# Router logits straight on the tokens, and the preparation of a group spread over thirteen tile steps instead of eleven

## What is computed

```python
xn = _layernorm(x, axis=-1)                     # x: 6250 tokens x 256
x = x + gnn(xn, src, dst, ...) + mix(xn[None], ...)[0]
x = x + ffn(_layernorm(x, axis=-1)[None], ...)[0]

def gnn(h, edge_row, edge_col, W, attn_fc, ln_gamma, ln_beta, ffn_w, ffn_b):
    # attention over 200000 edges gives h_new, then
    h_new = (h_new - mu) * rsqrt(var + eps) * ln_gamma + ln_beta
    return relu(h_new @ ffn_w + ffn_b)

def ffn(x, gamma, beta, Wr, br, W1, b1, W2, b2):  # 8 experts, 2 per token
    xn = (x - mu) * rsqrt(var + eps) * gamma + beta
    logits = einsum('bsd,de->bse', xn, Wr) + br
    top_vals, top_idx = top_k(logits, 2)
    w = softmax(top_vals)
    # y = sum over the two experts e of w_e * (gelu(xn @ W1[e] + b1[e]) @ W2[e] + b2[e])
```

## Time and profile before

| | us |
|---|---|
| timed runs, median of 3 (lowest to highest) | 4579.16 (4575.05 to 4580.97) |
| profiled execution, its own time | 4535.56 |
| span of that execution, first to last instruction | 4533.7 |
| mean granted TensorE clock | 0.82 |
| TensorE busy, in the whole span | 3115.7 (69%) |
| VectorE busy | 2756.3 (61%) |
| ScalarE busy | 1949.4 (43%) |
| GpSimd busy | 2177.1 (48%) |

### The profile page before, as it was taken

The page is one execution under the profiler, slowest core; times in us unless marked ns, Lnnn a source line. Parts: engine busy times, 40 slices in busy tenths (PEclk is TensorE's granted clock), DMA queues, the critical chain, the costliest instruction groups (busy, mean ns, idle before and its releaser), DMA issues.

```text
span 4533.7 us, 80190 instructions
## 1 busy us (share of the span) xinstructions
PE 3115.7 (69%) x17657; PEld 2171.6 (48%) x17657; DVE 2756.3 (61%) x6375; ACT 1949.4 (43%) x5742; POOL 2177.1 (48%) x2438
## 2 busy tenths in 40 slices
PE   4888366666676666677777677776776454777895
PEld 2443133333343433365555555555555333665785
DVE  8999866566676766665555565565555465434322
ACT  4777233233333333344444444444444222544674
POOL 5877555555555555554444444444443532123123
PEclk8888677787788887788888888887888777988998
DMA  2222333434444444433333333333332333334344
GB/s 67 98 96 88 93 102 102 108 102 101 116 108 104 121 100 107 112 93 88 83 83 86 84 91 84 92 88 82 88 83 77 94 113 131 109 106 150 96 137 135
DMA packets 326432, 452.92 MB, mean 100 GB/s; under 512 B 79021, under 2 KB 261483, under 8 KB 326053
## 3 DMA queue, kind: packets, MB, share of 16 engines
q0 software_dynamic: 85552, 236.37, 19.2%
q1 hardware_dynamic: 217896, 194.32, 14.9%
q10 hardware_dynamic: 22860, 20.83, 1.6%
HBM read 366.49 MB, written 84.82 MB: 100 GB/s over the span
## 4 chain that ended last, share of the span: by engine, by line
PE 26%; DVE 22%; issue 19%; another core or an unknown queue 16%; DVEq 7%; ACT 4%; POOL 2%; ACTq 1%; DMA 1%; SPq 1%; POOLq 0%
PE bank L2044 7%; DVE room L1580 4%; PE bank L2228 4%; PE bank L2240 4%; DVEq L1539 3%; PE bank L2078 2%; DVE room L1373 2%; DVE room L1563 2%; DVE room L1372 2%; PE bank L2089 2%; DVE room L1533 1%; DVE room L1553 1%; PE bank L2053 1%; ACT room L1174 1%
## 5 line engine op out<-in xcount | busy, mean ns | idle before, releaser
L883 POOL DMA_INDIRECT room<-table,room x1564 | 1521.1, 973 | 1558.2 <-DVE room L1563 1087.1
L2044 PE MATMUL bank<-room 128*128 128x260 f32 x3520 | 1053.2, 449 | 441.0 <-DVE room L1563 246.5
L2044 PEld LDWEIGHTS bank<-room 128*128 128x128 f32 x3520 | 750.0, 225 | 607.1 <-issue 484.1
L1563 DVE TENSOR_TENSOR room<-room,bank 128x1024 f32<-128x1024 f32 x440 | 534.3, 1214 | 68.5 <-issue 38.6
L1580 DVE TENSOR_TENSOR room<-bank,room 128x1024 f32<-128x1024 f32 x392 | 477.0, 1217 | 133.3 <-remote 69.5
L1174 ACT ACTIVATE room<-bank 128x512 f32<-128x512 f32 (+1 forms) x588 | 251.1, 487 | 372.1 <-remote 291.1
L1553 DVE TENSOR_REDUCE room<-bank 128x32 f32<-128x128 f32 x440 | 124.6, 283 | 438.0 <-remote 251.2
L1106 ACT ACTIVATE bank<-room 128x16 f32<-128x16 f32 x440 | 80.6, 183 | 683.3 <-DVE room L1557 429.9
L1099 ACT ACTIVATE spare<-away,ones 128x512 bf16<-128x512 bf16 x440 | 317.6, 722 | 56.1 <-ACT away L1096 7.9
L2053 PE MATMUL bank<-room 128*33 128x512 f32 (+1 forms) x1568 | 293.6, 480 | 41.6 <-issue 33.8
L2078 PE MATMUL bank<-ident,room 128*128 128x128 f32 x1764 | 296.0, 322 | 34.3 <-issue 23.1
(11 more groups left out here) (319 smaller groups left out, 4939.0 us busy)
## 6 DMA issues: line engine op xcount, KB each, us to landing
spare<-rows_dram SPq DMA_DIRECT2D x440, 128.0 KB
room<-table,room POOLq DMA_INDIRECT x1564
kv_dram<-room SPq DMA_DIRECT2D x49, 324.0 KB, 2.2
room<-kv_dram SPq DMA_DIRECT2D x196, 81.0 KB
y_dram<-planes SPq DMA_DIRECT2D x119, 128.0 KB
room<-xs_dram ACTq DMA_DIRECT2D x110, 128.0 KB
q_dram<-room SPq DMA_DIRECT2D x49, 192.0 KB, 1.9
room<-q_dram SPq DMA_DIRECT2D x196, 48.0 KB
```

The lines of the kernel that those rows point to most:

```text
L883: pool.indirect_dma_start(G[:, k.slot, u, :], None, table, bass.IndirectOffsetOnAxis(ap=ixbuf[:, k.slot, u:u + 1].bitcast(I32), axis=0)).t ...
L1563: dve.tensor_tensor(Gw[:, h, :, 0:C].rearrange("p u (h d) -> p u h d", h=GH), G[:, bass.ds(slot, 1), :, 0:C].rearrange("p a u (h d) -> p ( ...
L2044: ins = pe.matmul(pbank[1 + h][:, 0:TW], OH[:, s, u, :], Gw[:, h, u, :], start=(u == 0), stop=(u == U - 1))
```

## The change

Three things. The router's logits of a group are computed with the transposed tokens stationary and the router's weights moving, one accumulation of two for each tile of tokens, so that they come out as tokens by 8; ACT's copy and the seven transposes back are gone, and so is part 6 of TensorE. The router's bias is now a row on all partitions, added by VectorE where it only copied; for that `bt` is spread over a tile `bt_bb`. The bank of the logits is used in two halves in turn. Second, the variance of x1 is a part of its own (14), and in the head the choice of group 0 (part 6) comes before group 1's variance and its places (8) before group 1's norm. Third, the tables: groups begin at 0, 8, 16 and 0, 9, and VectorE's last part comes 13 steps after its first.

```diff
-    br = carve(1)
+    br = carve(XE)
@@
-    SKEW = {"dve": {0: 0, 10: 1, 1: 2, 3: 4, 11: 5, 4: 7, 6: 9, 7: 10, 8: 11}, "act": {2: 3, 5: 8, 7: 10}, "pe": {2: 3, 3: 4, 5: 8, 6: 9, 8: 10},
-            "pool": {0: 1, 3: 5, 80: 11, 82: 12, 84: 13, 86: 14}, "sp": {1: 1, 2: 4, 3: 7, 5: 8}}
-    BEGIN = {0: (0, 9, 18), 1: (0, 10)}
+    SKEW = {"dve": {0: 0, 10: 1, 1: 3, 3: 5, 11: 6, 14: 7, 4: 8, 6: 11, 7: 12, 8: 13}, "act": {2: 4, 5: 9, 7: 11}, "pe": {2: 4, 3: 5, 5: 9, 8: 12},
+            "pool": {0: 2, 3: 7, 80: 13, 82: 14, 84: 15, 86: 15}, "sp": {1: 1, 2: 5, 3: 7, 5: 8}}
+    BEGIN = {0: (0, 8, 16), 1: (0, 9)}
@@
-                due_parts[name][BOFF[b] + begins[-1] + 11].append((b + 1, "list"))
+                due_parts[name][BOFF[b] + begins[-1] + 13].append((b + 1, "list"))
             if name == "dve":
-                due_parts[name][BOFF[b] + begins[-1] + 12].append((b + 1, "places"))
+                due_parts[name][BOFF[b] + begins[-1] + 14].append((b + 1, "places"))
@@
     def log_bank(g):
-        return pbank[7 if g < BATCHES[0][1] else 2]
+        return pbank[7 if g < BATCHES[0][1] else 2][:, 256 * (g % 2):256 * (g % 2) + 256]
@@ ACT
-        def copy_logits(g):
-            act.wait_ge(logt_made, g + 1)
-            flat = lT[0:XE, :, :].rearrange("p a n -> p (a n)")
-            for hf in range(2):
-                o.mark(act.activation(flat[:, hf * (TOK // 2):(hf + 1) * (TOK // 2)], pbank[hf][0:XE, 0:TOK // 2], ACT.Identity, bias=br[0:XE, 0:1]))
-            o.settle()
-            act.sem_inc(log_copied, 1)
@@ VectorE, part 11
                 dve.sem_inc(x1_ready, 1)
 
+            if part == 14:
                 variance(g, gb, 1.0 + LN_EPS, LN_EPS * LN_EPS)
@@ VectorE, part 6
-                o.then(dve.tensor_copy(L, log_bank(g)[:, 0:GT * XE].rearrange("p (a e) -> p a e", a=GT)))
+                o.then(dve.tensor_tensor(L, log_bank(g)[:, 0:GT * XE].rearrange("p (a e) -> p a e", a=GT), br[:, :].unsqueeze(1).to_broadcast([P, GT, XE]), ALU.add))
@@ VectorE, the head
         o.mark(dve.tensor_copy(gn_bb[:, :, :], gn_b[:, :].unsqueeze(2).to_broadcast([P, 2, P])))
+        o.mark(dve.tensor_copy(bt_bb[:, :, :], bt[:, :].unsqueeze(2).to_broadcast([P, 2, P])))
@@
-        for g, part in ((0, 1), (1, 0), (1, 10), (0, 3), (1, 1), (0, 11), (1, 12), (0, 4), (1, 13), (1, 11), (1, 4), (0, 6), (0, 7), (0, 8), (1, 6), (1, 8)):
+        for g, part in ((0, 1), (1, 0), (1, 10), (0, 3), (1, 1), (0, 11), (0, 14), (1, 12), (0, 4), (1, 13), (1, 11), (0, 6), (1, 14), (0, 8), (1, 4), (0, 7), (1, 6), (1, 8)):
@@ TensorE, part 5, and part 6 gone
                 pe.wait_ge(tr_copied, (turn(g, 1) + 1) * 4)
-                for hf in range(2):
+                pe.wait_ge(ff_copied, max(g + 1, BATCHES[0][1]) * GT)
+                if g >= 2:
+                    pe.wait_ge(routed, g - 1)
+                for j in range(GT):
                     for c in range(2):
-                        ins = pe.matmul(pbank[hf][0:XE, 0:TOK // 2], wr[:, c, :], turned(g)[:, c, hf * (TOK // 2):(hf + 1) * (TOK // 2)],
-                                        start=(c == 0), stop=(c == 1))
-                ins.then_inc(logt_made, 1)
-            if part == 6:
-                pe.wait_ge(log_copied, g + 1)
-                pe.wait_ge(ff_copied, max(g + 1, BATCHES[0][1]) * GT)
-                if g:
-                    pe.wait_ge(routed, g)
-                for j in range(GT):
-                    ins = pe.transpose(log_bank(g)[:, j * XE:(j + 1) * XE], lT[0:XE, j, :], ident[0:XE, 0:XE])
+                        ins = pe.matmul(log_bank(g)[:, j * XE:(j + 1) * XE], turned(g)[:, c, j * P:(j + 1) * P], wr[:, c, :],
+                                        start=(c == 0), stop=(c == 1), skip_group_check=True)
                 ins.then_inc(log_made, 1)
```

More of the change, by code:

```diff
@@ L314, in _build @@
     assert used[0] - C - early_at >= 2 * GT * C
+    bt_bb = carve(2, P, at=early_at + 2 * GT * C)
+    assert early_at + 2 * GT * C + 2 * P <= used[0] - C
     g_b = [gb, carve(GT, C, at=early_at)]
@@ L601, in _ @@
         early += [(dst[:, :], t[name].rearrange("(c p) -> p c", p=P), s_w4) for dst, name in ((gn_g, "ln_gamma"), (gn_b, "ln_beta"), (gm, "gamma"), (bt, "beta"))]
-        early += [(br[0:XE, :], t["br"].rearrange("(n a) -> n a", a=1), s_w4)]
+        early += [(br[:, :], t["br"].partition_broadcast(P), s_w4)]
         early += [(w2[:, e, :, :], t["W2"][e].rearrange("(c p) n -> p c n", p=P), s_w4e) for e in range(XE)]
@@ L1912, in _ @@
             o.mark(dve.tensor_scalar(wr[:, c, :], wr[:, c, :], gm[:, c:c + 1], None, ALU.mult))
-        o.mark(dve.tensor_tensor(br[0:XE, :], br[0:XE, :], pbank[2][0:XE, C:C + 1], ALU.add))
+        o.mark(dve.tensor_tensor(br[:, :], br[:, :], pbank[2][:, C:C + XE], ALU.add))
         o.settle()
         dve.sem_inc(s_fold, 1)
-        for g, part in ((0, 1), (1, 0), (1, 10), (0, 3), (1, 1), (0, 11), (1, 12), (0, 4), (1, 13), (1, 11), (1, 4), (0, 6), (0, 7), (0, 8), (1, 6), (1, 8)):
+        for g, part in ((0, 1), (1, 0), (1, 10), (0, 3), (1, 1), (0, 11), (0, 14), (1, 12), (0, 4), (1, 13), (1, 11), (0, 6), (1, 14), (0, 8), (1, 4), (0, 7), (1, 6), (1, 8)):
             prepare(g, part)
@@ L2247, in _ @@
         for c in range(2):
-            ins = pe.matmul(pbank[2][0:XE, C:C + 1], wr[:, c, :], bt[:, c:c + 1], start=(c == 0), stop=(c == 1))
+            ins = pe.matmul(pbank[2][:, C:C + XE], bt_bb[:, c, :], wr[:, c, :], start=(c == 0), stop=(c == 1))
         ins.then_inc(s_fold, 1)
         pe.wait_ge(s_fold, 3)
-        for g, part in ((0, 2), (0, 3), (1, 2), (1, 3), (0, 5), (0, 6), (0, 8), (1, 5), (1, 6), (1, 8)):
+        for g, part in ((0, 2), (0, 3), (1, 2), (1, 3), (0, 5), (0, 8), (1, 5), (1, 8)):
             prepare(g, part)
```

3 lines of the change are left out of this document (removed).

## The result

The changed kernel takes 4591.4 us (median of 20 runs, 4557.6 to 4619.5) against 4577.1 of the kernel before (20 runs, 4521.7 to 4593.3). The ratio is 1.0051, 95% interval 1.003 to 1.0071: **slower by 0.5%, some 23 us**, where I had forecast 10 us less. The profiled execution after took 4583.8 us (span 4582.0).

The account below looks back on a forecast made before the run. It took TensorE's tiles at 3.74 us plus mostly waiting, some 43 us per woven-in group, as the bound. Head -2.0, first batch +1.7, second batch -10 sum to -10.3: 4568.9 us, own range 4560 to 4577, overall 4548 to 4596.

Parts of the forecast that it names:

- Logits, "I take 3.1": TensorE's logits of a group, 28 load-and-matmul pairs: 1.8 to 3.1 us, taken as 3.1, against 5.1 the old way.
- rival (c): Does less than forecast: logits cost 5.9 at 0.21 per pair, SP decides the head, second batch gets 4; 4577, chance 0.16.
- Head, -2.0: Before the first tile: first scatter 3.2 us earlier, last of 28 2.4 earlier, so the head 2.0 us shorter.
- Its pace unchanged: In the head, SP's eight clearing DMAs, 1.2 us later, still take 21.7; if they end last, +1.4 us.
- First batch, +1.7: First batch with groups 2 to 4 woven in: 258.1 us against 256.4, no gain per group.
- my cycles of 59.5 and 69.7: First batch's laid-out new cycles of eight tiles: 59.5 us without scatters, 69.7 with them.
- The hold of the scatters, 10.2: In a woven-in group, the scatter run starts with `ff` and holds the next tile, +10.2 us; old cycle +10.5.
- Second batch, -10: Groups 5 and 6: power ahead of the scatters, group 6's transposes at 48.6 and not 60.4; 10 us less.
- Rival (b), +16 by scatters on `ff`: Scatter run holds TensorE from its first us, 10.7 more for groups 2, 3 and 5; about +16, 4595, chance 0.22.
- Transfer to the median: Profiled execution 4535.56, timed median 4579.16, 0.96% above and unexplained; the difference of -10.3 was moved over to the median.

Follow-up runs that it names:

- e1: Changed kernel with the tables (group starts and steps) of the kernel before, keeping new logits and new head order; 1.0057 of the kernel before.
- e8: Changed kernel with each of the 28 logits matmuls moving 128 columns instead of 8; 1.0010 of the kernel before.
- e2: Kernel before with only the new order in the head, old logits and old tables; 1.0008 of the kernel before.
- e3: Changed kernel with the old form of the logits, under the new tables and new head; 1.0038 of the kernel before.
- e14: Kernel before with only the scatters of groups 2, 3 and 5 spaced in four portions; 0.9928 of the kernel before.
- e7: e3 with places, scatters and list one step earlier (step 12); 0.9991 of the kernel before.
- e9: e8 with places, scatters and list one step earlier (step 12); 0.9977 of the kernel before.
- e10: e9 with ScalarE's exponential one step later (12) and VectorE's weights at step 13; 0.9938 of the kernel before.
- e12: e10 with the old form of the logits; 0.9961 of the kernel before.
- e6: Changed kernel with the 28 logits matmuls of groups 2 to 6 issued in pairs between the next tile's matmuls; 1.0072 of the kernel before.

## Why the prediction was wrong, point by point

- **Logits, "I take 3.1".** This is the step that failed. I bounded a pair of load and matmul by rows of the full clock (0.065 and 0.112) and took the clock for given: that the new matmuls could lower it is no term of the sum. Measured: 6.14 for 28 in three of seven groups (the expectation of e1 says four, a miscount), 3.86 to 5.33 in the others, that is 0.14 to 0.22 each; the price that I gave rival (c), 0.21, was about right (6.14 / 28 = 0.22), though no row stood behind it, but as a whole that rival stopped at the logits. What it left out is larger: the clock stays down for the tile behind. Together 18.6 us in the first condition (e8) and 17.4 in the second (e1 against e2). The two batches came out 33.5 above their forecast (25.2 and not -8.3): 18.6 of it is this, the other 15 are the tables (+6.4 and not -8.3), below. The 3.1 itself was good for loads and columns at the full clock: 3.39 in e8.
- **Head, -2.0.** Seen -4.9, and not by my reckoning. The first scatter is 2.9 earlier against the head's start (65.2 against 68.1; I said 3.2). But the last of 28 is 2.7 later and not 2.4 earlier, and still the first tile comes 5.8 earlier, since it was SP's clearing that ended last: it starts 2.9 later and takes 13.02 and not the 21.73 of the earlier trace rows. "Its pace unchanged" was the wrong assumption, and so was that the slow pace ends with the scatters: in the kernel before 9.0 of the 21.73 us lie behind the last scatter (3812.6), and after, nearly all 13.02 lie beside scatters (the last ends at 3844.3). What sets the pace is open. SyncE's queue after:

```profile
3831.72 13.02 SPq L680 DMA_DIRECT2D xs_dram<-room  x8
```

  In the first condition all eight profiles with the new head have 120.8 to 123.7, the two with the old one 126.1 and 126.3.
- **First batch, +1.7.** Seen +14.7. The waits came, most of them smaller than laid out: 1.1 to 2.3 before the second transposes (I said 2.1), 2.17 for norm 1 (I said 2.7), 1.7 to 1.9 for ScalarE (3.5), 4.08 for places (4); my cycles of 59.5 and 69.7 were 65.9 and 71.9. What is missing is the clock: in the first cycle the logits take 6.14 and not 3.1, the tile behind the third chunk 3.52 and not 1.95, `ff` 7.98 and not the 6.1 for which I had given the slow clock only where scatters ran. e8 takes the logits' clock away and leaves +6.6; e3 puts the tables' price, without any standing, at 10.6.
- **The hold of the scatters, 10.2, the same in both kernels.** Right in size (12.0 by e14), and in the changed kernel it fell on the tile, as I had it. But I misread whom it holds in the kernel before. It is `ff` there, and not the tile "that suffered": TensorE's timeline of before has the tile whole at 1.95 and 8 of the 28 matmuls of `ff` through before the 9.84 of idle time in the earlier trace rows; in the next cycle it is 9.10, in the second batch 13.80.

```profile
3902.67 1.95 PE L2228 MATMUL bank<-room 128*128 128x128 f32 x16
...
3906.19 1.89 PE L2185 MATMUL bank<-room,row_step 128*128 128x256 f32 x8
```

  The timeline of after, all engines, in the middle of the run:

```profile
3950.36 0.27 PE L2216 MATMUL bank<-room 128*128 128x128 f32 x1 [0.64 <-issue]
...
3951.77 0.27 PE L2216 MATMUL bank<-room 128*128 128x128 f32 x1 [1.15 <-issue]
3952.20 0.96 POOL L942 DMA_INDIRECT xs_dram<-agg,room  x1 [0.30 <-issue]
...
3956.98 0.42 DVE L1874 TENSOR_TENSOR planes<-bank,spare 128x256 f32<-128x256 f32 x1 [11.76 <-remote]
```

- **Second batch, -10.** Seen +10.5. Two things were wrong. The transposes of group 6 came 54.6 after the `ff` end of group 5 and not 48.6 (logits 6.14 and the tile behind them are in between), so scatters started at 59.9 and not 52.9, and the tile behind `ff` was held until 93.3 where I had 80.8 (before, where the hold is on `ff`: 95.4). And I had looked only at groups 5 and 6 against each other: group 5's own first transposes are now one step later and meet the first gathers of the batch, which hold them too. TensorE's timeline after:

```profile
4125.52 1.04 PE L2162 MATMUL bank<-ident,room 128*128 128x128 f32 x8
4132.59 1.12 PE L2162 MATMUL bank<-ident,room 128*128 128x128 f32 x4 [6.02 <-issue]
```

  From read-out 35 to group 5's `ff` end it is 25.8 and not 16.5; 3.7 of these 9.3 are the one tile more that the tables put there. By e8 the tables alone are worth +0.1 in this batch, where I had -10.
- **Rival (b), +16 by scatters on `ff`,** would have given the right time for the wrong reason: in the changed kernel `ff` is whole in every group (7.98 and 6.63 at a stretch). A run on `ff` would be nothing new either: it is what the kernel before has in groups 3, 4 and 6. In e7, e9, e10 and e12 it came in group 6.
- **Transfer to the median.** Moving the difference over was sound in kind; but a part of it is a spread before the last stage (28.9 between two profiles) that no profile of a single run can foretell.

## What to carry to other kernels

Price a replacement on TensorE also by what it leaves of the clock: here 28 weight loads with 8 moving columns each cost more than their own time, namely the next tile at 1.2 GHz, and widening the moving side, which looks like waste, was faster than that (and about as fast as the old form). Spreading them among long ones spared a clock that was up and prolonged one that was down. When a table spreads steps, write down for every step which engine waits in the same step for a result of that step: here two such meetings, places with `ff` and the exponential with the choice, cost about as much as the wait that was spread. And break up runs of indirect DMAs where other engines stand during them: on the kernel before that alone was worth 0.7%, in the condition in which they stand.

## What the runs showed of the hardware

- **A block of matmuls with few moving columns takes TensorE's clock down, with TensorE busy all the while.** 28 pairs with 8 columns: clock 0.74 over the stretch in e1, 1.00 with 128 columns in the same place (e8). Spread among long matmuls (e6) they left the clock as they found it: at 1.00 in two groups, at the lower level in three (0.51 over 21 us). The Trainium skill, TensorE: Matmul & The Clock Gate, section HAM oscillation — how this bites in real kernels, tells of a clock lost by idle gaps; here TensorE is busy 11.8 of 13.2 us in e1's stretch, so gaps don't explain e1, while the clock of e6's three groups fell behind gaps of 2.5 to 5.6 us.
- **Engines stand during a run of indirect DMAs, in one condition and not in the other.** Runs of 14 held TensorE, VectorE and ScalarE (releaser "remote" or "issue", TensorE's matmuls coming singly, mostly with 0.2 to 1.2 us between them); runs of four did so much less (72.1 and 25.4 us of "remote" before VectorE's instructions, before and e14). In the second condition the same 14, at the same 1.27 us each, hold nobody (0.0). The Trainium skill, SBUF — State Buffer, section Who interferes with whom, says that a DMA never contends with a compute engine; here engines stood beside DMAs that GpSimd issues all the same. Whether that is contention for the memory, of which the page speaks, or something else, such as instructions that come late to the engines, no run here shows.
- **The same condition seems to make the difference ahead of the last stage.** Of the 1033 us between the profiles of the kernel before in the two conditions 964 lie before the last stage. TensorE's matmuls of line L2044 between 1500 and 2500 us, kernel before in the first condition and in the second:

```profile
L2044 PE MATMUL bank<-room 128*128 128x260 f32 x1104 | 325.2, 444 | 116.3 <-issue 59.5 <-DVE room L1563 56.8
```
```profile
L2044 PE MATMUL bank<-room 128*128 128x260 f32 x1528 | 368.9, 385 | 12.8 <-issue 12.8
```

  In the same 1000 us it gets 1104 done and not 1528, with 59.5 of idle time of the kind "issue" against 12.8; the edge loop issues 1564 indirect DMAs. That this is one cause with the hold is argued, not shown. It is no matter of the kernel, which is the same in both.
